# A decoder layer on one core: the first transposes of both attentions moved from TensorE to transposing DMAs

## The chip, the core and the metric

The kernel runs on one core of a Trainium2 chip. The metric is the device time of one execution in microseconds (us), lower is better. Engines by name: TensorE (PE; its weight loads are PEld), VectorE (DVE), ScalarE (ACT), GpSimd (POOL) and SyncE (SP), which here only issues DMAs. SBUF is the memory of 128 partitions that all engines work in, PSUM the one that TensorE writes to, in 8 banks.

## What is computed

One decoder layer on x, 16 batches of 128 tokens with 256 features, float32:

```
x = layernorm(x + differential_self_attention(x))   # 16 heads of 16, each split into two halves of 8
x = layernorm(x + cross_attention(x, ctx))          # 32 query heads of 8 over 8 key/value heads
x = layernorm(x + mixture_of_experts(x))            # 8 experts, 2 chosen per token, 2 shared ones
```

In the self attention queries and keys are rotated, each head's two halves give a softmax of their own, and the second is subtracted times a scalar lambda. Either attention therefore has 32 score matrices of 128 x 128 for a batch, with a depth of only 8:

```
scores = einsum(q, k) * scale (+ add_mask);  p = softmax(scores);  out = p @ v
```

## The kernel before

**Split numbers.** Float32 products are made from float16 pieces: a value is split into a high part (ScalarE, a cast) and a low part (GpSimd, the value less its high part). For a batch, the queries of an attention `t` (A self, C cross) lie in the tile `t.qs`, [128 tokens, 32 heads, 32 slots] f16: high, low, high, and one slot for the negated row maximum. The keys lie in `t.ks` in the same way. So a tile is 128 x 1024 f16, 256 KB.

**Two passes.** Scores are computed twice. `max_scores` (L942) makes them in 8 fills of 4 heads, VectorE takes the row maximum of each (`largest`, L678) and writes it into the query tile. Then the queries are transposed again, now with the maxima in them (`restack`, L936), and `exp_scores` (L955) computes scores less maximum, on which ScalarE takes the exponential (`exp`, L512). Both passes read tiles with the head dimension on the partitions: `t.qm` the queries of the first pass, `t.qt` those of the second, `t.kt` the keys of both.

**The transposes.** `stack_T` (L914) makes such a tile with 8 transposes of 128 x 128 on TensorE into one PSUM bank; ScalarE or VectorE copies the bank to SBUF (`qm_in`, `kt_in`, `reqt_in`). There are six for a batch: first queries, keys and second queries, for each attention. `stack_q` (L922) and `stack_k` (L930) are the first ones of queries and keys.

**The order.** The attention block is a software pipeline. Each engine has a function `body(n)`, written out by hand, that is run for n = 0 to 22; iteration n holds steps of several batches at once: x is projected and rotated for batch n, the first pass of the self attention is at batch n - 1, its second pass at n - 2, its output at n - 3, the cross attention's second pass at n - 4, and so on. The engines meet only at semaphores. PSUM banks are shared in rings: `RINGS` (L50) lists for each bank, or pair of banks, which results take turns in it, and `Turns.wait` makes TensorE wait until the result before has been read. The transposes of both attentions have turns in the single banks 4 and 5, with the projections and the routing.

In an iteration TensorE does, among the rest and in this order: `stack_q(A, n-1)` after the first scores of the second pass, `stack_k(A, n-1)`, `restack(C, n-4)`, `out_project(n-3)`, `max_scores(A, n-1, 0)`, ..., `values_cross(n-4, 0)`, `stack_k(C, n-3)`, `project_qk(n)`, `stack_q(C, n-3)`, `group_mean(n-2)`, `values_cross(n-4, 1)`, `restack(A, n-1)`, `max_scores(C, n-3, 0)`. `keep_warm` adds matmuls without a use where TensorE would idle, in the first and last iterations. GpSimd's low parts are `q_low` (L306), `k_low` (L312), `cross_k_low` (L324), `cross_q_low` (L318).

**SyncE.** It issues the loads at the start, then two pieces of the shared experts' weights, fills the DRAM tensor `xs` (39 tiles of 128 rows) with zeros by one DMA, loads four more weight pieces as their buffers come free, and waits for the zeros. The experts' part follows after the attention block, and the change doesn't touch it.

Of the kernel before, what the change touches and what calls it, by code (L numbers as in the profile page):

```python
# [56 lines left out]
    (1, (("aqT", 1, 0), ("akT", 1, 0), ("v", 1, 0), ("xT", 0, 0), ("qk", 0, 0), ("are", 1, 0))),  # L57
    (1, (("rt", 7, 0), ("cre", 4, 0), ("x2T", 6, 0), ("ckT", 3, 0), ("cqT", 3, 0))),
# [5 lines left out]
SHARED_HIGH = 3  # L64
LAST = B + 1
# [44 lines left out]
def build(nc, a, out):  # L110
    ctx = ExitStack()
    sems = ExitStack()
    with sems, ctx:
# [31 lines left out]
        def attention_tiles(p, vheads):  # L145
# [3 lines left out]
            t.qm, t.qt, t.kt = (sb(p + n, [P, NC, P], F16) for n in ("qm", "qt", "kt"))  # L149
# [9 lines left out]
            t.s_qT, t.s_kT, t.s_reT = sem(p + "qT"), sem(p + "kT"), sem(p + "reT")  # L159
# [70 lines left out]
        def live(b):  # L230
# [6 lines left out]
            "aqT": (A.s_qm_in, 1), "akT": (A.s_kt_in, 1), "are": (A.s_reqt, 1),  # L237
            "cqT": (C.s_qm_in, 1), "ckT": (C.s_kt_in, 1), "cre": (C.s_reqt, 1), "x2T": (A.s_x2lo, 1), "rt": (A.s_lgc, 1),
# [14 lines left out]
        def _(sp):  # L253
# [13 lines left out]
            sp.dma_start(x_all[:, 4:B, :], xv[:, 4:B, :]).then_inc(s_x[2], 16)  # L267

            sp.wait_ge(s_set, 4)
            for k in range(2):  # L270
                load_piece(sp, NE * 3 + k, k)
            sp.wait_ge(s_pset, 11)
            sp.dma_start(zero[:, E:E + 1], a["pad_row"]).then_inc(s_rowno, 16)
            sp.dma_start(x_row[:, :, E], a["acc_row"], allow_slow_non_contiguous=True).then_inc(s_rowno, 16)
            sp.wait_ge(s_rowno, 32)
            sp.dma_start(xs.rearrange("(n p) c -> p n c", p=P),
                         zero[:].unsqueeze(1).to_broadcast([P, TILES, RW])).then_inc(s_zero, 16)
            for k in range(2, NSH * 3):
                sp.wait_ge(s_xwlo, k - 1)
                load_piece(sp, NE * 3 + k, k)  # L280
            sp.wait_ge(s_zero, 16)
# [149 lines left out]
        def _(act):  # L431
# [34 lines left out]
            def k_high(b):  # L466

                act.activation(A.ks[:, :, 0:2 * SD].rearrange("p j (r d) -> p j r d", d=SD),
                               A.rq[:, E:2 * E].rearrange("p (j d) -> p j d", d=SD).unsqueeze(2)
                               .to_broadcast([P, SUB, 2, SD]), ACT.Copy).then_inc(A.s_khi, 1)  # L470
# [10 lines left out]
            def cross_k_high(b):  # L481

                if b == 0:
                    act.wait_ge(s_ctx, 16)
                else:
                    act.wait_ge(C.s_kT, b)
# [4 lines left out]

            def qm_in(t, one, b):

                act.wait_ge(t.s_qT, b + 1)
                act.activation(t.qm[:].rearrange("p c n -> p (c n)"), one.bitcast(F16), ACT.Copy
                               ).then_inc(t.s_qm_in, 1)

            def kt_in(t, one, b):

                act.wait_ge(t.s_kT, b + 1)  # L500
                if b:
                    act.wait_ge(t.s_expfill, FILLS * b)
                act.activation(t.kt[:].rearrange("p c n -> p (c n)"), one.bitcast(F16), ACT.Copy
                               ).then_inc(t.s_kt_in, 1)
# [30 lines left out]
            def body(n):  # L535
# [18 lines left out]
                if live(n - 1):  # L554
                    kt_in(A, a_one, n - 1)
# [22 lines left out]
                if live(n - 3):  # L578
                    cross_q_high(n - 3)
                    if n < LAST:  # L580
                        kt_in(C, c_one, n - 3)
# [3 lines left out]
                if live(n - 3) and n < LAST:  # L585
                    qm_in(C, c_one, n - 3)
# [15 lines left out]
        def _(dve):  # L602
# [57 lines left out]

            def qm_in(t, one, b):

                dve.wait_ge(t.s_qT, b + 1)
                dve.tensor_copy(t.qm[:].rearrange("p c n -> p (c n)"), one.bitcast(F16)).then_inc(t.s_qm_in, 1)

            def kt_in(t, one, b):

                dve.wait_ge(t.s_kT, b + 1)
                if b:
                    dve.wait_ge(t.s_expfill, FILLS * b)  # L670
                dve.tensor_copy(t.kt[:].rearrange("p c n -> p (c n)"), one.bitcast(F16)).then_inc(t.s_kt_in, 1)
# [115 lines left out]
            def body(n):  # L787
# [8 lines left out]
                if live(n - 1):  # L796
                    qm_in(A, a_one, n - 1)
# [45 lines left out]
                if live(n - 3) and n >= LAST:  # L843
                    kt_in(C, c_one, n - 3)
# [16 lines left out]
                if live(n - 3) and n >= LAST:  # L861
                    qm_in(C, c_one, n - 3)
# [13 lines left out]
        def _(pe):  # L876
# [45 lines left out]
            def stack_q(t, one, b):  # L922
# [3 lines left out]
                pe.wait_ge(t.s_qlo, b + 1)  # L926
                turns.wait(pe, "aqT" if t is A else "cqT", b)
                stack_T(t.qs, one, t.s_qT)

            def stack_k(t, one, b):  # L930

                pe.wait_ge(t.s_klo, b + 1)
                turns.wait(pe, "akT" if t is A else "ckT", b)
                stack_T(t.ks, one, t.s_kT)

            def restack(t, one, b):  # L936

# [4 lines left out]
            def max_scores(t, b, f):  # L942

                if f == 0:
                    pe.wait_ge(t.s_qm_in, b + 1)
                    pe.wait_ge(t.s_kt_in, b + 1)
                turns.wait(pe, "am" if t is A else "cm", b, f)
                r = slice(SLOTS * (f % 4), SLOTS * (f % 4) + USED)
                for j in range(NI):
                    c = NI * (f // 4) + j  # L950
                    ins = pe.matmul(score_bank(t, "m", b, f)[:, j * P:(j + 1) * P], t.qm[r, c, :], t.kt[r, c, :],  # L951
# [956 lines left out]
```

## Time and profile before

| | |
|---|---|
| median of 3 runs | 839.91 us (838.23 to 842.63) |
| the profiled execution | 839.69 us, its span 837.6 us |
| TensorE busy | 774.1 us, 92% |
| VectorE, ScalarE busy | 524.6 us (63%), 516.2 us (62%) |
| GpSimd busy | 309.3 us, 37% |
| mean granted clock of TensorE | 0.976 |

The span is the time from the first to the last instruction of the profiled execution; what its own time has more lies around it. Busy shares are means over both parts of the kernel, the attention block and the experts. The attention block ends at about 426 us.

### The profile page before, as it was taken

Reading aid. Unit: us, or ns where it says so; the run is one execution under the profiler, and the core shown is the slowest. Engines: PE = TensorE matmul, PEld = TensorE weight load, DVE = VectorE, ACT = ScalarE, POOL = GpSimd, SP = SyncE. Lnnn points to the kernel's source line nnn. Section 1 sums busy time; section 2 is a strip of 40 time slices with the busy share of each in tenths; the row PEclk is TensorE's granted clock in tenths of the full one; section 3 lists DMA queues with packets and bytes.
Section 4 is the critical chain, followed back from the end, with each engine's and each line's share of the span. In section 5 each row is a group of like instructions: output and inputs, shape, how many; then the busy total and the mean of one; then the engine's idle time right before and its main releaser. Section 6 shows DMA issues by size and latency. Waiting matters only on the chain. (4 is left out here: it accounts for less than half of the span.)

```text
span 837.6 us, 20147 instructions
## 1 busy us (share of the span) xinstructions
PE 774.1 (92%) x7698; PEld 512.9 (61%) x7698; DVE 524.6 (63%) x1193; ACT 516.2 (62%) x944; POOL 309.3 (37%) x480
## 2 busy tenths in 40 slices
PE   7888999999999999988889899989999999999993
PEld 5555555555555555555545555658888887788652
DVE  3346788888888888876448866764444444444353
ACT  2445788888888888774425554545565555565443
POOL 3134445555555555555200683002222222222222
PEclk9997999999999999999899999999999999999997
DMA  8900000001010100000033685432233233233321
GB/s 247 250 3 1 2 2 33 2 2 33 3 33 2 33 2 3 2 2 1 2 98 126 197 244 164 164 101 33 46 53 46 46 50 48 46 51 46 59 100 63
DMA packets 38282, 51.02 MB, mean 61 GB/s; under 512 B 9264, under 2 KB 33072, under 8 KB 38192
## 3 DMA queue, kind: packets, MB, share of 16 engines
q1 hardware_dynamic: 31040, 40.39, 16.3%
q0 software_dynamic: 7152, 9.34, 6.8%
q8 instruction: 66, 1.08, 0.5%
q14 instruction: 24, 0.20, 0.1%
HBM read 31.04 MB, written 18.68 MB: 59 GB/s over the span
## 5 line engine op out<-in xcount | busy, mean ns | idle before, releaser
L1392 POOL DMA_INDIRECT acc<-y_sb,xin x39 | 60.6, 1553 | 217.8 <-ACT y_sb L1460 217.8
L1713 PE MATMUL ps<-wr,xr_hi 128*128 x624 | 129.3, 299 | 0.0
L1431 ACT ACTIVATE th<-ps 128x384 f32<-128x384 f32 (+1 forms) x118 | 58.0, 491 | 109.8 <-PE ps L1713 104.9
L1713 PE MATMUL ps<-xg_hi,wsh 128*128 128x512 f16 x320 | 102.6, 383 | 4.6 <-DVE xg_lo L1578 4.6
L682 DVE TENSOR_REDUCE a_qs<-ps 128x4 f16<-128x512 f32 x128 | 85.2, 690 | 18.8 <-PE ps L951 17.9
L682 DVE TENSOR_REDUCE c_qs<-ps 128x4 f16<-128x512 f32 x128 | 84.4, 694 | 16.7 <-PE ps L951 15.3
L515 ACT ACTIVATE a_pt<-ps 128x512 f32<-128x512 f32 x128 | 74.7, 596 | 31.4 <-PE ps L968 29.5
L1713 PE MATMUL ps<-wr,xr_lo 128*128 x312 | 93.4, 299 | 0.0
L1585 DVE SCALAR_TENSOR_TENSOR th<-th,ps 128x384 f32<-128x384 f32 (+1 forms) x118 | 65.3, 554 | 33.4 <-ACT th L1431 33.2
L515 ACT ACTIVATE c_pt<-ps 128x512 f32<-128x512 f32 x128 | 69.7, 603 | 21.1 <-PE ps L968 20.8
L1672 DVE COPY ht<-ps 128x512 f16<-128x512 f16 x39 | 16.6, 425 | 94.0 <-PE ps L1792 94.0
L1713 PE MATMUL ps<-wr,ht 128*128 x585 | 70.5, 273 | 0.8 <-issue 0.7
L1713 PEld LDWEIGHTS ps<-wr,xr_hi 128*128 128x128 f16 x624 | 59.4, 98 | 18.2
L1713 PEld LDWEIGHTS ps<-wr,ht 128*128 128x128 f16 x585 | 56.8, 98 | 8.5 <-issue 1.6
L1713 PE MATMUL ps<-xg_lo,wsh 128*128 128x512 f16 x160 | 61.3, 383 | 0.0
L1713 PE MATMUL ps<-wsh,ht_hi 128*128 128x256 f16 x320 | 54.7, 273 | 3.7 <-DVE ht_lo L1590 3.4
L1590 DVE TENSOR_TENSOR hs<-th,hs 128x384 f16<-128x384 f32 x78 | 38.4, 492 | 29.0 <-ACT hs L1436 29.0
L1436 ACT ACTIVATE hs<-th 128x384 f16<-128x384 f32 x78 | 36.6, 470 | 31.9 <-DVE th L1585 31.9
L1713 PEld LDWEIGHTS ps<-xg_hi,wsh 128*128 128x128 f16 x320 | 31.6, 99 | 39.9 <-issue 5.9
L962 PE MATMUL ps<-mask,id 128*128 128x512 f16 x128 | 50.9, 398 | 3.3 <-ACT a_qt L509 3.3
L968 PE MATMUL ps<-a_qt,a_kt 32*128 32x128 f16 x512 | 51.8, 222 | 0.0
L968 PEld LDWEIGHTS ps<-a_qt,a_kt 32*128 32x128 f16 x512 | 29.2, 94 | 33.5 <-issue 33.5
(214 smaller groups left out, 1758.3 us busy)
## 6 DMA issues: line engine op xcount, KB each, us to landing
wst<-in_wx SPq DMA_DIRECT2D x30, 640.0 KB, 4.4
xs<-zero SPq DMA_DIRECT2D x1, 5031.0 KB, 19.8
xin<-xs SPq DMA_DIRECT2D x39, 129.0 KB, 2.1
acc<-x_row SPq DMA_DIRECT2D x4, 512.0 KB, 3.3
x_row<-acc SPq DMA_DIRECT2D x8, 256.0 KB, 5.2
out<-x_row SPq DMA_DIRECT2D x8, 256.0 KB, 2.1
x_row<-in_x SPq DMA_DIRECT2D x1, 1536.0 KB, 10.9
wst<-in_wqkvT SPq DMA_DIRECT2D x1, 768.0 KB, 4.3
```

Of the source, the lines that this page charges most:

```text
L515: act.activation(t.pt[:, f, :, :].rearrange("p j n -> p (j n)"), score_bank(t, "e", b, f), ACT.Exp, scale=(E // HEADS if t is A else SD) * ...
L682: dve.tensor_reduce(t.qs[:].rearrange("p (c i) s -> p c i s", i=NI)[:, c:c + 4, f % 4, USED], score_bank(t, "m", b, f).rearrange("p (j n) ...
L962: pe.matmul(o.rearrange("p (j n) -> p j n", j=NI), id16[:], mask4[:].unsqueeze(1).to_broadcast([P, NI, P]), start=True, stop=False, skip_g ...
L968: ins = pe.matmul(o[:, j * P:(j + 1) * P], t.kt[r, c, :], t.qt[r, c, :], start=t is C, stop=True, skip_group_check=t is A)
L1392: pool.indirect_dma_start(acc, bass.IndirectOffsetOnAxis(ap=row, axis=0), y_sb[:, n % 2, :], None, compute_op=ALU.add).then_inc(f_acc, 16)
L1431: act.activation(th[:, k % 2, 0:n], gate[:, k % 2, 0:n], ACT.Silu, scale=1.0 / WSCALE).then_inc(f_th, 1)
L1436: act.activation(dst, th[:, k % 2, 0:dst.shape[-1]], ACT.Copy).then_inc(f_hhi, 1)
L1585: dve.scalar_tensor_tensor(out=t, in0=t, scalar=1.0 / WSCALE, in1=up[:, k % 2, 0:n], op0=ALU.mult, op1=ALU.mult).then_inc(f_hid, 1)
L1590: dve.tensor_tensor(dst, th[:, k % 2, 0:dst.shape[-1]], hi, ALU.subtract).then_inc(f_hlo, 1)
L1672: dve.tensor_copy(ht[:, HALVES[1][0]:, :, :].rearrange("p j r n -> p (j r n)"), htp[1]).then_inc(f_hTin[1], 1)
L1713: ins = pe.matmul(o, l[x], r[y], start=(first and n == 0), stop=(last and n == m - 1), skip_group_check=not (first and last))
```

## The change

The first transposes of queries and keys, in both attentions, are made by a transposing DMA from SBUF to SBUF, issued by SyncE. The second transposes of the queries stay on TensorE. `qm_in` and `kt_in` and their turns in the banks are gone. `t.kt` has two buffers, taken by even and odd batches. SyncE now has a `body(n)` as the other engines do; the load of x for batches 4 to 15, the pieces of shared weights and the zeros, now 13 DMAs of 3 tiles, are issued between the transposes.

```diff
-    (1, (("aqT", 1, 0), ("akT", 1, 0), ("v", 1, 0), ("xT", 0, 0), ("qk", 0, 0), ("are", 1, 0))),
-    (1, (("rt", 7, 0), ("cre", 4, 0), ("x2T", 6, 0), ("ckT", 3, 0), ("cqT", 3, 0))),
+    (1, (("v", 1, 0), ("xT", 0, 0), ("qk", 0, 0), ("are", 1, 0))),
+    (1, (("rt", 7, 0), ("cre", 4, 0), ("x2T", 6, 0))),
...
+ZT = 3
...
-            t.qm, t.qt, t.kt = (sb(p + n, [P, NC, P], F16) for n in ("qm", "qt", "kt"))
+            t.qm, t.qt = (sb(p + n, [P, NC, P], F16) for n in ("qm", "qt"))
+            t.kt = sb(p + "kt", [P, 2, NC, P], F16)
...
-            sp.dma_start(x_all[:, 4:B, :], xv[:, 4:B, :]).then_inc(s_x[2], 16)
...
+            def turn(dst, src, done):
+                sp.dma_start_transpose(out=dst, in_=src[:].rearrange("p j s -> p (j s)")).then_inc(done, 16)
+            def stack_k(t, b):
+                sp.wait_ge(t.s_klo, b + 1)
+                if b >= 2:
+                    sp.wait_ge(t.s_expfill, FILLS * (b - 1))
+                turn(t.kt[:, b % 2, :, :], t.ks, t.s_kt_in)
+            def stack_q(t, b):
+                sp.wait_ge(t.s_qlo, b + 1)
+                if b:
+                    sp.wait_ge(t.s_maxfill, FILLS * b)
+                turn(t.qm[:], t.qs, t.s_qm_in)
...
+            def zero_rows(k):
+                if k == 0:
+                    sp.wait_ge(s_rowno, 32)
+                ts = slice(k * ZT, (k + 1) * ZT)
+                sp.dma_start(xs.rearrange("(n p) c -> p n c", p=P)[:, ts, :],
+                             zero[:].unsqueeze(1).to_broadcast([P, ZT, RW])).then_inc(s_zero, 16)
+            def shared_piece(k):
+                if k < 2:
+                    sp.wait_ge(s_set, 4)
+                else:
+                    sp.wait_ge(s_xwlo, k - 1)
                 load_piece(sp, NE * 3 + k, k)
...
+            def body(n):
+                if live(n - 1):
+                    stack_q(A, n - 1)
+                if live(n - 1):
+                    stack_k(A, n - 1)
+                if n == 1:
+                    sp.dma_start(x_all[:, 4:B, :], xv[:, 4:B, :]).then_inc(s_x[2], 16)
+                if live(n - 3):
+                    stack_k(C, n - 3)
+                if n == 2:
+                    shared_piece(0)
+                    shared_piece(1)
+                    row_numbers()
+                k, half = divmod(n - SHARED_HIGH, 2)
+                if half == 0 and 2 <= k < NSH * 3:
+                    shared_piece(k)
+                if 0 <= n - 3 < TILES // ZT:
+                    zero_rows(n - 3)
+                if live(n - 3):
+                    stack_q(C, n - 3)
```

The high parts of the next batch wait for the DMA that reads the key tile, where they waited for the transposes (`act.wait_ge(A.s_kt_in, 16 * b)` in `k_high`, and the same in `cross_k_high`). `max_scores(t, b, 0)` waits for both DMAs. The calls of `stack_q`, `stack_k`, `qm_in` and `kt_in` are taken out of the bodies of TensorE, ScalarE and VectorE; all else there keeps its place.

## Rows read from the trace of the kernel before

**Rows 1.** The page: span, busy time and its 40 slices.

```profile
span 837.6 us, 20147 instructions
...
PE 774.1 (92%) x7698; PEld 512.9 (61%) x7698; DVE 524.6 (63%) x1193; ACT 516.2 (62%) x944; POOL 309.3 (37%) x480
...
PEclk9997999999999999999899999999999999999997
```

**Rows 2.** Windows of 21 us: length, busy us (instructions) of each engine, PEclk, DMA share.

```profile
63.00:84.00 21.00, 18.00 (x170) 10.58 (x162) 13.92 (x33) 11.15 (x19) 8.81 (x17) 0.75 0.01 1
210.00:231.00 21.00, 19.76 (x274) 12.36 (x275) 17.55 (x43) 17.36 (x33) 11.25 (x20) 1.00 0.01 3
```

**Rows 3.** Timeline of GpSimd, the rotary sum of batches 4 and 15: start, us.

```profile
99.74 1.27 POOL L304 TENSOR_TENSOR a_rq<-a_rq,a_r 128x512 f32<-128x512 f32 x1
...
344.48 1.26 POOL L304 TENSOR_TENSOR a_rq<-a_rq,a_r 128x512 f32<-128x512 f32 x1
```

**Rows 4.** Timeline of TensorE in one steady iteration, matmuls only.

```profile
264.46 0.41 PE L951 MATMUL ps<-a_kt,a_qm 24*128 24x128 f16 x8
...
276.94 0.40 PE L951 MATMUL ps<-c_kt,c_qm 24*128 24x128 f16 x8
...
281.46 0.62 PE L919 MATMUL ps<-id,a_qs 128*128 128x128 f16 x8
281.92 0.38 PE L962 MATMUL ps<-mask,id 128*128 128x512 f16 x1
...
283.23 0.62 PE L919 MATMUL ps<-id,a_ks 128*128 128x128 f16 x8
...
286.70 0.41 PE L951 MATMUL ps<-a_kt,a_qm 24*128 24x128 f16 x8
```

**Rows 5.** Timeline of GpSimd in the same iteration: the low parts.

```profile
272.30 0.63 POOL L321 TENSOR_TENSOR c_qs<-x_row,c_qs 128x256 f16<-128x256 f32 x1 [0.82 <-ACT c_qs L477]
...
280.73 0.67 POOL L309 TENSOR_TENSOR a_qs<-a_rq,a_qs 128x256 f16<-128x256 f32 x1 [0.80 <-ACT a_qs L462]
...
281.55 0.67 POOL L315 TENSOR_TENSOR a_ks<-a_rq,a_ks 128x256 f16<-128x256 f32 x1
...
287.77 0.67 POOL L327 TENSOR_TENSOR c_ks<-ctx_all,c_ks 128x256 f16<-128x256 f32 x1 [4.76 <-ACT c_ks L488]
```

**Rows 6.** Timelines of ScalarE and VectorE in the same iteration: the copies out of PSUM.

```profile
272.90 1.02 ACT L503 ACTIVATE c_kt<-ps 128x1024 f16<-128x1024 f16 x1 [0.68 <-PE ps L968]
...
274.87 1.02 ACT L495 ACTIVATE c_qm<-ps 128x1024 f16<-128x1024 f16 x1
...
285.57 1.02 ACT L503 ACTIVATE a_kt<-ps 128x1024 f16<-128x1024 f16 x1
...
282.12 0.69 DVE L664 COPY a_qm<-ps 128x1024 f16<-128x1024 f16 x1 [0.35 <-PE ps L919]
```

**Rows 7.** The page, DMA issues: KB each, median us from issue to landing.

```profile
wst<-in_wx SPq DMA_DIRECT2D x30, 640.0 KB, 4.4
xs<-zero SPq DMA_DIRECT2D x1, 5031.0 KB, 19.8
...
x_row<-acc SPq DMA_DIRECT2D x8, 256.0 KB, 5.2
out<-x_row SPq DMA_DIRECT2D x8, 256.0 KB, 2.1
```

**Rows 8.** DMA view of 0 to 430 us, same columns.

```profile
wst<-in_woT SPq DMA_DIRECT2D x1, 256.0 KB, 3.5
...
ones<-in_ones SPq DMA_DIRECT2D x1, 32.0 KB, 1.9
...
x_row<-in_acc_row SPq DMA_DIRECT2D x1, 8.0 KB, 7.2
```

**Rows 9.** Timeline of SyncE's queue: start, and us that the issue itself took.

```profile
0.73 0.40 SPq L255 DMA_DIRECT2D x_row<-in_x  x1
...
8.46 1.90 SPq L267 DMA_DIRECT2D x_row<-in_x  x1
```

More of the change, by code:

```diff
@@ L236, in build @@
             "xT": (A.s_xlo, 1), "qk": (A.s_rdve, 3), "v": (A.s_vin, 1),
-            "aqT": (A.s_qm_in, 1), "akT": (A.s_kt_in, 1), "are": (A.s_reqt, 1),
-            "cqT": (C.s_qm_in, 1), "ckT": (C.s_kt_in, 1), "cre": (C.s_reqt, 1), "x2T": (A.s_x2lo, 1), "rt": (A.s_lgc, 1),
+            "are": (A.s_reqt, 1),
+            "cre": (C.s_reqt, 1), "x2T": (A.s_x2lo, 1), "rt": (A.s_lgc, 1),
             "apv0": (A.s_ot[0], 1), "apv1": (A.s_ot[1], 1), "cpv0": (C.s_ot[0], 1), "cpv1": (C.s_ot[1], 1),
@@ L266, in _ @@
             sp.dma_start(ctx_all[:], a["ctx"].rearrange("(b p) c -> p b c", p=P)).then_inc(s_ctx, 16)
-            sp.dma_start(x_all[:, 4:B, :], xv[:, 4:B, :]).then_inc(s_x[2], 16)
-            sp.wait_ge(s_set, 4)
-            for k in range(2):
-                load_piece(sp, NE * 3 + k, k)
-            sp.wait_ge(s_pset, 11)
-            sp.dma_start(zero[:, E:E + 1], a["pad_row"]).then_inc(s_rowno, 16)
-            sp.dma_start(x_row[:, :, E], a["acc_row"], allow_slow_non_contiguous=True).then_inc(s_rowno, 16)
@@ L275, in _ @@
[L275 to L281, printed above, removed]
+            def turn(dst, src, done):
+                sp.dma_start_transpose(out=dst, in_=src[:].rearrange("p j s -> p (j s)")).then_inc(done, 16)
@@ new lines, in stack_k, with row_numbers @@
+            def stack_k(t, b):
[8 more added lines that the diff above has]
+                turn(t.qm[:], t.qs, t.s_qm_in)
+            def row_numbers():
+                sp.wait_ge(s_pset, 11)
+                sp.dma_start(zero[:, E:E + 1], a["pad_row"]).then_inc(s_rowno, 16)
+                sp.dma_start(x_row[:, :, E], a["acc_row"], allow_slow_non_contiguous=True).then_inc(s_rowno, 16)
@@ L284, in _ @@
+            for n in range(ITERATIONS):
+                body(n)
+            sp.wait_ge(s_zero, 16 * TILES // ZT)
         @block.gpsimd
@@ L466, in k_high @@
             def k_high(b):
+                if b:
+                    act.wait_ge(A.s_kt_in, 16 * b)
                 act.activation(A.ks[:, :, 0:2 * SD].rearrange("p j (r d) -> p j r d", d=SD),
@@ L485, in cross_k_high @@
                 else:
-                    act.wait_ge(C.s_kT, b)
+                    act.wait_ge(C.s_kt_in, 16 * b)
                 for r in range(2):
@@ L490, in cross_k_high @@
                                    .to_broadcast([P, KV, GRP, SD]), ACT.Copy).then_inc(C.s_khi, 1)
[L492 to L504, printed above, removed]
             def reqt_in(t, one, b):
@@ L584, in body @@
                     exp(C, n - 4, 7)
-                if live(n - 3) and n < LAST:
-                    qm_in(C, c_one, n - 3)
                 if live(n - 4):
@@ L659, in rope_second @@
                                   ).then_inc(A.s_rdve, 1)
[L661 to L671, printed above, removed]
             def reqt_in(t, one, b):
@@ L842, in body @@
                     moments(A, A.bn, A.mv, n - 2, A.s_bn, A.s_mv)
-                if live(n - 3) and n >= LAST:
-                    kt_in(C, c_one, n - 3)
                 if live(n - 1):
@@ L860, in body @@
                     cross_moments(n - 5)
-                if live(n - 3) and n >= LAST:
-                    qm_in(C, c_one, n - 3)
                 if live(n):
@@ L920, in stack_T, with restack @@
                 ins.then_inc(s, 1)
-            def stack_q(t, one, b):
+            def restack(t, one, b):
                 if t is A and b == 0:
                     pe.wait_ge(s_const, 16 * N_CONST)
[L926 to L936, printed above, removed]
                 pe.wait_ge(t.s_maxed, FILLS * b + FILLS)
@@ L944, in max_scores @@
                 if f == 0:
-                    pe.wait_ge(t.s_qm_in, b + 1)
-                    pe.wait_ge(t.s_kt_in, b + 1)
+                    pe.wait_ge(t.s_qm_in, 16 * b + 16)
+                    pe.wait_ge(t.s_kt_in, 16 * b + 16)
                 turns.wait(pe, "am" if t is A else "cm", b, f)
```

20 lines of the change are left out of this document (3 added, 17 removed).

## The prediction

> **What bounds the kernel now.** I read the page first: TensorE is busy 92% of the span, VectorE and ScalarE little over 60%, and its granted clock is full nearly throughout [rows 1]. The change lies in the attention block alone, the first half of the span, so I went on to windows of that block. In a steady one of 21 us TensorE is busy 19.8, VectorE 17.6, ScalarE 17.4 [rows 2]: TensorE bounds it, but the other two have only 3.5 us to spare, so a wait put into the chain between them can't hide for long. The rotary sum of batch 4 starts at 99.74 and that of batch 15 at 344.48 [rows 3]: 11 iterations of 22.25 us. With the neighbours that are nearly as full, I count 13 steady iterations. Four batches are in flight, but every engine runs a fixed order, so the iteration is a ring of dependent steps, and I measured that ring with the timelines of one iteration [rows 4, 5]:
>
> - (a) cross max scores start 276.94, the low part of the self keys ends 281.55 + 0.67 = 282.22: 5.3 us
> - (b) from there to the self max scores at 286.70: 4.5 us
> - (c) self max scores at 264.46 to the end of the low part of the cross queries, 272.30 + 0.63 = 272.93: 8.5 us
> - (d) from there to the cross max scores at 276.94: 4.0 us
>
> The sum is 22.3, the period. In (b) and (d) a transpose and its copy out of PSUM are done today, between other work. These two gaps, 8.5 us together, are the room that a transposing DMA has before the period grows.
>
> **What is removed.** Four of the six transpose groups of an iteration leave TensorE. One occupies it from 281.46 to 281.92 [rows 4], 0.46 us for 8 transposes; four are 1.83 us. Three copies of 1.02 us leave ScalarE and one of 0.69 us leaves VectorE [rows 6]: with overlap about 2.8 and 0.6 us. With nothing waiting for a DMA, TensorE's own period would be 22.23 - 1.83 = 20.4: VectorE then has 18.6 - 0.6 = 18.0 of work (17.6 x 22.2/21 = 18.6) and ScalarE 15.6, so TensorE stays the bound. I split TensorE's work so: (a) + (b) less the two self groups, 9.76 - 0.92 = 8.8 us; (c) + (d) less the two cross groups, 12.48 - 0.92 = 11.6 us.
>
> **What is added.** Four DMAs an iteration on SyncE's queue, each 128 x 1024 f16, 256 KB. The trace has no transposing DMA, so landing time (L) and issue time (I) are bounded by its plain ones. L: 256 KB out of SBUF to HBM land in 2.1 us, 256 KB into SBUF in 5.2 (behind other traffic) and, as the weights of the projection, in 3.5 [rows 7, 8]. I take 3.3, close to the latter, a little less since nothing is queued ahead. I: the shortest issue takes 0.40 us, that of a load in 1,536 rows of 1 KB takes 1.90 [rows 9]; a transpose of 1,024 rows of 256 B lies between, I take 1.4. Waits in the order of SyncE's program: self queries (low part over at 280.73 + 0.67 = 281.40), then self keys (ready at 282.22), then cross keys (ready 288.44 [rows 5], wanted a full 10 us later: hidden), then cross queries. So the self keys are issued behind the self queries: issue 1.4 less the 0.8 between them is 0.6 us late. Gap (b) becomes L + 0.6 = 3.9, gap (d) L = 3.3. What waits there is TensorE at its first max scores, all in its order behind them (the values, the scores of the other attention, the next projection), and through them VectorE's maxima and ScalarE's exponentials.
>
> In (a) a late start no longer waits behind the second transpose's copy, and VectorE and ScalarE have no backlog: I shorten it by 0.4, to 4.9. In (c) VectorE's maxima run as before: 8.5, and 0.1 for the semaphore. The period is then the larger of 8.8 and 4.9 + 3.9 = 8.8, plus the larger of 11.6 and 8.6 + 3.3 = 11.9: 20.7. Gain 22.23 - 20.7 = 1.53; 13 x 1.53 = 19.9 us.
>
> The Trainium skill ("DMA: Bandwidth & Descriptors", Latency and other measured facts and its table of limits) gives a transposing DMA 261 GB/s, and some 2 us fixed for any DMA (Anatomy of one DMA). My estimate from that page is 1.0 + 2.0 = 3.0 us for 256 KB; the sum by it would be 20.4 a period, 4 us better in all. No row here shows a transposing DMA.
>
> **What moves.** The write of zeros was one DMA, 5,031 KB in 19.8 us [rows 7]; it is now 13 pieces of 387 KB, by the same row 1.5 us each, issued between cross keys and cross queries in 13 iterations. Alone it is done (288.5 + 1.4 + 1.5) long before the cross queries at 295.2. In four iterations a shared weight piece of 4.4 us [rows 7] stands ahead of it: 288.5 + 1.4 + 4.4 + 1.5 = 295.8, so the transposes behind it start up to a microsecond late: 4 x 1.0 = 4 us. (If the zeros held it up each time: 13 x 1.5 = 20 us; if never, 0.) The shared pieces are loaded later than before, but are used only at the end of the iteration: hidden. x of batches 4 to 15 goes behind the first two transposes; batch 4 is wanted three iterations on: nothing. The doubled key tile only takes away a wait. Start and drain: iterations 1 and 16 to 18 are chains of latency, where TensorE's transpose and copy took less than a DMA does; about 1 us later in two of them: 2 us. The experts are as before: 0.
>
> **Sum.** 839.7 (the profiled execution, span 837.6; the median of runs is 839.9) - 19.9 + 4 + 2 = 825.8: 826.
>
> **The rivals.**
>
> 1. *All hidden.* L is like the store's 2.1 us [rows 7], I near 0.4: period 20.4, 13 x 1.83 = 23.8, start and contention 1: 817. For it: a transpose reads and writes SBUF only. Against: every load in the rows took over 3 us for this size.
> 2. *A draw.* L = 3.9, still I = 1.4: 4.9 + 4.5 plus 8.6 + 3.9 = 21.9 a period; 13 x 0.33 = 4.3 gained, 6 lost: 841. This is the point from which it decides: above L of 3.7 nothing is left of the gain.
> 3. *Slower, TensorE waits for small pieces.* A DMA pays by the piece. The 8 KB of row numbers go in 2,048 pieces, 128 for each of 16 engines, in 7.2 us [rows 8]; against 1.9 for 32 KB of ones in the same rows that is 5.3/128 = 41 ns a piece. A transpose has 1,024 rows of 256 B, 64 to an engine: 64 x 41 ns = 2.6 us, L = 1.9 + 2.6 = 4.5, and the keys follow the queries 2.6 - 0.8 = 1.8 later. 4.9 + 6.3 plus 8.6 + 4.5 = 24.3: 13 x 2.1 = 27 lost, plus 6: 872. For it: those pieces did cost that. Against: they are 4 bytes each and strided in HBM. Waits of 2 us could also drop TensorE's clock, as in the window from 63 us, where it was busy only 18.0 us and was granted 0.75 [rows 2], that is half speed for half of the window; 3 us at half speed in each iteration would cost 13 x 1.5 = 20 us more, 892.
> 4. *Far slower, square block by square block.* A transpose is eight blocks of 128 x 128, 32 KB each; a 32 KB load takes 1.9 us [rows 8]. One after another they take up to 15 us, the keys 14 us behind: 4.9 + 29 plus 8.6 + 15 = 58 a period, 1,300 us. The Trainium skill ("VectorE: DVE Perf Modes", The three transpose paths) speaks against the change: it gives 1,309 ns for one such block by DMA, 390 on TensorE, and advises TensorE where the result may lie in PSUM. My estimate by that page is 8 x 1.3 = 10.5 us, a period of 44 and 1,125 us. Against: nothing says that the blocks don't overlap.
>
> **The numbers.** This kernel's runs spread over 838.2 to 842.6, so about 0.5% (4.2 us) is what can be told from no change. Chances: forecast 0.36 (its own range 819 to 835), rival 1 0.14, rival 2 0.14, rival 3 0.31, rival 4 0.05. Faster 0.50, same 0.14, slower 0.36. For 8 in 10 the range leaves out rival 4, the upper part of rival 3 with the clock, and a little of rival 1: 814 to 880.
>
> **What would show it.** Landing of the transposes in the DMA issues: under 3.7 right, over 3.9 wrong. Rotary sums 20.7 us apart. TensorE waiting for the queue at the max scores: about 0.3 us before the cross ones, near nothing before the self ones; if a microsecond or more stands before both, rival 3. Groups of L919 down from 768 to 256 matmuls, ScalarE's busy time down by some 44 us. The granted clock of the steady windows still 1.00. The prediction is wrong if the issue occupies SyncE for over 2 us, if a transpose holds up the DMAs around it, or if the ring was not (a) to (d).

## The result: a small gain where a larger one was forecast

The changed kernel takes 835.91 us in the median of 20 runs (828.14 to 840.4), the kernel before, beside it, 840.51 us (834.29 to 846.55). The ratio is 0.9936, interval 0.9909 to 0.9962: 0.6% faster, 4.6 us by the medians and 5.4 by the ratio. Forecast were 826 and a gain of 14. The profiled execution of the changed kernel took 836.23 us, its span 834.1. In two kernels below, e3_self_only and e7_edges_warm, one and two of 12 runs were in a slower state at a lower clock; those runs are left out below.

The page of the changed kernel: span, busy time of TensorE and ScalarE, TensorE's granted clock in 40 slices, against [rows 1].

```profile
span 834.1 us, 19099 instructions
...
PE 759.6 (91%) x7186; PEld 491.4 (59%) x7186; DVE 510.3 (61%) x1173; ACT 474.4 (57%) x900; POOL 309.9 (37%) x480
...
PEclk9787799999999999996699999999999999999998
```

ScalarE lost 41.8 us and VectorE 14.3. TensorE has 512 matmuls fewer, but the clock row shows 7, 8, 7, 7 in the second to fifth slices (9, 9, 7, 9 before) and 6, 6 in the two at the end of the attention block (9, 8 before). The execution's mean clock is 0.951 against 0.976.

The DMA issues of the changed kernel (KB each, median us from issue to landing), against [rows 7].

```profile
wst<-in_wx SPq DMA_DIRECT2D x30, 640.0 KB, 4.7
xs<-zero SPq DMA_DIRECT2D x13, 387.0 KB, 4.1
...
a_qm<-a_qs SPq DMA_TRANSPOSE x16, 3.2
a_kt<-a_ks SPq DMA_TRANSPOSE x16, 3.1
c_kt<-c_ks SPq DMA_TRANSPOSE x16, 3.5
c_qm<-c_qs SPq DMA_TRANSPOSE x16, 3.0
```

A transpose of 128 x 1024 f16 lands in 3.0 to 3.2 us in the median of three of the four kinds, and in 3.5 for the cross keys, whose issue itself often took longer. A piece of zeros took 4.1 us. SyncE's queue in one steady iteration (start, us of the issue):

```profile
254.24 1.23 SPq L272 DMA_TRANSPOSE a_qm<-a_qs  x1
255.57 1.29 SPq L272 DMA_TRANSPOSE a_kt<-a_ks  x1
259.71 2.51 SPq L272 DMA_TRANSPOSE c_kt<-c_ks  x1
262.27 0.57 SPq L299 DMA_DIRECT2D xs<-zero  x1
267.32 1.23 SPq L272 DMA_TRANSPOSE c_qm<-c_qs  x1
```

Timelines of GpSimd: the rotary sums of batches 1, 4 and 15 and, in between, the low parts of self keys and cross queries in that iteration, against [rows 3, 5].

```profile
31.96 1.27 POOL L357 TENSOR_TENSOR a_rq<-a_rq,a_r 128x512 f32<-128x512 f32 x1 [15.55 <-DVE a_r L685]
...
103.48 1.26 POOL L357 TENSOR_TENSOR a_rq<-a_rq,a_r 128x512 f32<-128x512 f32 x1
...
254.35 0.67 POOL L368 TENSOR_TENSOR a_ks<-a_rq,a_ks 128x256 f16<-128x256 f32 x1
...
266.66 0.64 POOL L374 TENSOR_TENSOR c_qs<-x_row,c_qs 128x256 f16<-128x256 f32 x1 [0.82 <-ACT c_qs L532]
...
334.56 1.26 POOL L357 TENSOR_TENSOR a_rq<-a_rq,a_r 128x512 f32<-128x512 f32 x1
```

From batch 4 to batch 15 the sums stand 231.08 / 11 = 21.0 us apart, each step between 20.98 and 21.18, against 22.25. So the steady part gained 13.7 us. The same rows tell where it went. Batch 4 starts 3.7 us later than in [rows 3]. Batch 0 starts 0.2 us later (13.02 against 12.80) and batch 1 4.5 us (31.96 against 27.42), so 4.3 us are lost between these two, and 0.8 are won back before batch 4. The end is the routing's softmax of the last batch, on VectorE, first of the kernel before:

```profile
426.09 0.24 DVE L1647 TENSOR_SCALAR sg<-lg 128x128 f32<-128x128 f32 x1 [0.33 <-PEq L1199]
```

and of the changed kernel:

```profile
420.98 0.24 DVE L1644 TENSOR_SCALAR sg<-lg 128x128 f32<-128x128 f32 x1 [0.33 <-PEq L1196]
```

From batch 15 to there it was 81.6 us and is 86.4: the drain lost 4.8. In all -13.7 + 3.7 + 4.8 = -5.1 us for the attention block (rounded). The experts, which the change leaves alone, took 1.6 us more in this execution (413.1 against 411.5).

**The steady iteration.** TensorE of the changed kernel, the rows that bound the ring, with the waits behind brackets, against [rows 4]:

```profile
254.52 0.39 PE L967 MATMUL ps<-mask,id 128*128 128x512 f16 x1 [0.36 <-ACT a_pt L556]
...
258.83 0.41 PE L956 MATMUL ps<-a_kt,a_qm 24*128 24x128 f16 x8
...
269.19 1.06 PE L1001 MATMUL ps<-c_pt,c_v 128*32 128x512 f32 x8 [0.68 <-DVE a_g L755]
...
270.75 0.41 PE L956 MATMUL ps<-c_kt,c_qm 24*128 24x128 f16 x8
```

No max scores wait here, neither the self ones at 258.83 nor the cross ones at 270.75. What TensorE waits for is ScalarE's exponential and VectorE's group statistics. Windows of one whole period show the account: before,

```profile
210.00:232.23 22.23, 20.99 (x284) 12.75 (x282) 18.78 (x47) 18.59 (x35) 12.19 (x23) 1.00 0.01 3
```

and after:

```profile
210.00:230.99 20.99, 19.21 (x251) 10.95 (x252) 18.00 (x46) 15.76 (x32) 12.16 (x23) 1.00 0.37 70
```

TensorE lost 1.78 us of work, about the 1.83 that were forecast, and its idle time grew from 1.24 to 1.78 us. The period shrank by the difference, 1.24.

**The edges.** In the attention block TensorE waits for a queue in only three places behind the first loads. They are the first self max scores and the cross max scores of batches 14 and 15:

```profile
20.66 0.41 PE L956 MATMUL ps<-a_kt,a_qm 24*128 24x128 f16 x8 [4.08 <-DMA a_kt<-a_ks]
...
374.61 0.41 PE L956 MATMUL ps<-c_kt,c_qm 24*128 24x128 f16 x8 [2.81 <-DMA c_qm<-c_qs]
...
394.15 0.62 PE L956 MATMUL ps<-c_kt,c_qm 24*128 24x128 f16 x8 [2.91 <-DMA c_qm<-c_qs]
```

Windows around them (length, busy us and instructions of each engine, PEclk, DMA share, GB/s), before:

```profile
20.00:30.00 10.00, 8.29 (x77) 5.69 (x78) 6.11 (x12) 1.79 (x3) 1.27 (x1) 1.00 0.81 217
...
390.00:400.00 10.00, 9.11 (x70) 5.25 (x69) 3.89 (x12) 3.93 (x8) 5.10 (x7) 0.72 0.01 2
400.00:410.00 10.00, 8.06 (x85) 5.17 (x84) 7.36 (x15) 2.17 (x4) 2.17 (x4) 0.84 0.01 2
```

and after:

```profile
20.00:30.00 10.00, 9.09 (x54) 4.78 (x55) 5.42 (x9) 0.77 (x2) 0.00 (x0) 0.56 0.50 157
...
63.00:84.00 21.00, 17.10 (x164) 9.53 (x166) 13.79 (x33) 9.63 (x18) 9.46 (x18) 0.73 0.27 60
210.00:231.00 21.00, 19.22 (x251) 10.96 (x252) 18.01 (x46) 15.77 (x32) 12.17 (x23) 1.00 0.37 70
...
390.00:400.00 10.00, 6.56 (x58) 3.36 (x56) 2.95 (x5) 2.46 (x5) 2.80 (x5) 0.67 0.15 28
400.00:410.00 10.00, 9.81 (x67) 5.96 (x69) 4.78 (x13) 3.19 (x7) 1.41 (x3) 0.50 0.00 0
```

Right behind the first wait the granted clock falls from 1.00 to 0.56: TensorE is busier there than before (9.09 against 8.29 us) and finishes 54 instructions instead of 77. The steady window stays at 1.00, and the dip of 63 to 84 us was there before (0.73 now, 0.75 in [rows 2]).

How much longer the wait itself became is read from the end of a low part to the max scores that need it. At the start, before (low part of the self keys, then the self max scores):

```profile
15.52 0.67 POOL L315 TENSOR_TENSOR a_ks<-a_rq,a_ks 128x256 f16<-128x256 f32 x1
...
19.03 0.41 PE L951 MATMUL ps<-a_kt,a_qm 24*128 24x128 f16 x8 [0.39 <-ACT a_kt L503]
```

and after, where the max scores are the row at 20.66 above:

```profile
15.74 0.67 POOL L368 TENSOR_TENSOR a_ks<-a_rq,a_ks 128x256 f16<-128x256 f32 x1
```

That is 2.84 us before and 4.25 after, 1.4 more. For cross batch 14, before and after (the max scores after are the row at 374.61):

```profile
381.16 0.67 POOL L321 TENSOR_TENSOR c_qs<-x_row,c_qs 128x256 f16<-128x256 f32 x1 [0.88 <-ACT c_qs L477]
...
384.38 0.41 PE L951 MATMUL ps<-c_kt,c_qm 24*128 24x128 f16 x8 [0.96 <-DVE c_qm L664]
```

```profile
370.82 0.67 POOL L374 TENSOR_TENSOR c_qs<-x_row,c_qs 128x256 f16<-128x256 f32 x1 [0.90 <-ACT c_qs L532]
```

This is 2.55 and 3.12 us, 0.6 more; for batch 15 it is 3.52 and 3.14, 0.4 less. So the three paths grew by 1.6 us together, though TensorE idles in them for 9.8 us: what it did there before (transposes, matmuls of `keep_warm`) overlapped them.

**Theories.** A: the steady part is worth what it shows, and the edges take it back, each wait by its own length and by the lower clock behind it. B: the steady gain is limited by the landing of the self keys or the cross queries. C: the moved loads and the zeros cost something of themselves. The first four kernels were aimed at A and at the split between the attentions, the next four at B and C and at a better version, the last three at A once more, by adding the waits to the kernel before.

### The profile page after: what moved, and what is told of

Same layout as the page of the kernel before. It is cut to its first block and busy times, and to the rows that moved or that the text cites. A ratio compares the mean times of both kernels' runs of the same rounds, so it can differ in the third digit from the quotient of the medians.

```text
span 834.1 us, 19099 instructions
## 1 busy us (share of the span) xinstructions
PE 759.6 (91%) x7186; PEld 491.4 (59%) x7186; DVE 510.3 (61%) x1173; ACT 474.4 (57%) x900; POOL 309.9 (37%) x480
## 5 line engine op out<-in xcount | busy, mean ns | idle before, releaser
L556 ACT ACTIVATE c_pt<-ps 128x512 f32<-128x512 f32 x128 | 69.8, 603 | 22.3 <-PE ps L973 21.6
```

The costliest lines, as they stand in the source:

```text
L556: act.activation(t.pt[:, f, :, :].rearrange("p j n -> p (j n)"), score_bank(t, "e", b, f), ACT.Exp, scale=(E // HEADS if t is A else SD) * ...
```

## Experiments on the edges and on each attention alone

For four of these kernels the first transposes can be put back on TensorE batch by batch. The core of the edit; the copies `qm_in` and `kt_in`, and the turns in the PSUM rings, are those of the kernel before:

```diff
+def on_pe(p, kind, b):
+
+    return 0 <= b < B and (...)
...
             def stack_k(t, b):
 
+                if on_pe(t.p, "k", b):
+                    return
                 sp.wait_ge(t.s_klo, b + 1)
...
                     exp_scores(A, n - 2, 5)
+                if on_pe("a", "k", n - 1):
+                    stack_k(A, a_one, n - 1)
```

**e1_warm: more matmuls of no use ahead of the three waits.**

```diff
                 if n == 1:
-                    keep_warm(8)
+                    keep_warm(8 + 30)
...
                 if n >= LAST and live(n - 3):
+                    keep_warm(24, a_one)
                     max_scores(C, n - 3, 0)
```

> The changed kernel, with 30 more warming matmuls ahead of the first self max scores and 24 more ahead of the cross max scores of the last two batches, the three places where its trace shows TensorE waiting for a transposing DMA (4.1, 2.8 and 2.9 us). Theory A: the waits cost most through the clock, which falls to half after them; filled, the clock stays at 2.4 GHz, the three waits still last, and the time falls by about 5 us against the changed kernel, to some 831 us (0.988 of the kernel before); the second rotary sum comes at 29 to 30 us in place of 32.0. Theory B: the waits cost by their own length only; nothing is gained, 0.994.

Measured: 837.3 us (829.46 to 840.22, 12 runs) against 841.94 of the kernel before; ratio 0.9942 (0.9905 to 0.9978), the same as for the change itself. The three waits shrank to 1.7, 1.1 and 0.4 us (a new one, of 1.5 us for the self queries, stood before the self max scores of batch 15). At the start this did not help: the window of 20 to 30 us still had a low clock, 0.60, and batch 1 started at 32.42. In the drain it did, in the one trace: from batch 15 to the end the granted clock was 0.92 and the time 84.0 us, against 0.82 and 86.4 in the change. That execution's attention block ended 3.5 us sooner than the change's, at 417.46, but its experts, which are the same in both, took 4.6 us longer, for no reason found. The mean clock rose to 0.964 in the average of the runs (0.956 for the change), without a gain in the whole time. The 5 us that theory A expected are not there, and filling the first wait this far was not enough.

**e2_edges: no transposing DMA at the edges.** `on_pe` is true for self batch 0 and for cross batches 14 and 15.

```diff
+    return 0 <= b < B and ((p == "a" and b == 0) or (p == "c" and b >= B - 2))
```

> The changed kernel with the first transposes of self batch 0 and of cross batches 14 and 15 given back to TensorE and their copies; all others by DMA. Theory A (the steady iterations gained 13.7 us, and start and drain gave back 3.7 and 4.8): the second rotary sum at 27.5 us, the attention block over at about 413 us, 0.984 of the kernel before, 827 us. Theory B (what is lost at the start and at the end comes of the moved loads and zeros on the same queue, or of the shorter steady iteration itself): the block is over at 418 us or later, 0.990 or more.

Measured: 829.52 us (826.45 to 831.74, 6 runs), ratio 0.987 (0.9828 to 0.9912). TensorE waits for no queue; batch 1 starts 14.71 us behind batch 0 (14.62 in the kernel before, 18.94 in the change), the steady steps are 20.99, the block ends at 414.40. So the three waits of the change are worth 5 to 6 us of its time (by the ratios 5.5, and 5.0 with e11_edges_again below). One iteration of the profiled execution took 25.49 us instead of 21, with this in its windows:

```profile
120.00:123.00 3.00, 2.69 (x37) 1.28 (x33) 2.69 (x5) 2.64 (x6) 2.19 (x6) 1.00 0.00 0
123.00:133.00 10.00, 9.87 (x74) 5.41 (x78) 5.53 (x14) 3.83 (x9) 3.89 (x7) 0.51 0.43 85
```

No queue was waited for there: the clock can fall in a steady iteration too, and this fall cost 4.5 us.

**e3_self_only and e4_cross_only: one attention by DMA.**

```diff
+    return 0 <= b < B and (p == "c")
```

for the self attention by DMA alone, and for the cross attention alone:

```diff
+    return 0 <= b < B and (p == "a")
```

> Only the self attention's first transposes by DMA, the cross ones on TensorE as before. If TensorE's work sets the period: 0.92 us off it, 21.3 us an iteration. If a ring of dependent steps sets it, whose gaps shrank only where a DMA took the place of transpose and copy: near 21.6. One wait of 4.1 us at the start stays, so 0.991 to 0.995 of the kernel before.

> Only the cross attention's first transposes by DMA. TensorE's work: 21.3 us a period; ring: near 21.7. The two waits in the drain stay (4.8 us given back), the start is as before: 0.992 to 0.997 of the kernel before.

Measured: e3_self_only 836.12 us (833.48 to 843.66, 11 runs), ratio 0.9967 (0.9934 to 1.0), steady steps mostly of 21.55 us; e4_cross_only 839.92 us (837.01 to 844.32, 12 runs), ratio 0.9983 (0.9955 to 1.001), steps of 21.74 and 21.84. Against 22.23 that is 0.68 and about 0.44 us for the halves, and 1.24 for both: within 0.12 the halves add up. Both are nearer to what the ring gave (21.6 and 21.7) than to the 21.3 of TensorE's work. In the whole time neither half can be told from no change with certainty: both intervals reach 1.0. The self half pays its wait of 4.0 us at the start, the cross half its two in the drain, 5.7 us together.

## Experiments on what sets the steady period

**e5_late_keys: the self keys 1.3 us later.**

```diff
                 if live(n - 1):
                     stack_q(A, n - 1)
+                if 5 <= n <= 14:
+                    sp.wait_ge(s_spare, 16 * (n - 5))
+                    sp.dma_start_transpose(out=spare[:], in_=wq_hi[:].rearrange("p c n -> p (c n)")[:, 0:NC * P]
+                                           ).then_inc(s_spare, 16)
                 if live(n - 1):
                     stack_k(A, n - 1)
```

> The changed kernel with one more transposing DMA of the same size (128 x 1024 f16, of constant weights into a spare tile) on SyncE's queue between those of the self queries and the self keys, in iterations 5 to 14. The self keys are then issued 1.2 to 1.3 us later. Theory (the ring through the landing of the self keys sets the period): the rotary sums of these iterations stand 22.2 us apart instead of 20.99, and TensorE shows a wait, perhaps not named as one for the queue, of about 1.2 us more before the self max scores. Rival (TensorE's own work sets the period, and the landing has slack): the period grows by less than 0.4 us. The whole kernel by the theory: 10 x 1.2 = 12 us more, about 848.

Measured: one run, 846.02 us, with steps of 22.3 us (22.26 to 22.40). In its timeline TensorE now waits before the self max scores:

```profile
222.12 0.41 PE L962 MATMUL ps<-a_kt,a_qm 24*128 24x128 f16 x8 [1.20 <-issue]
```

The keys were issued 2.70 us behind the queries instead of 1.33, so 1.37 later. Of that 1.20 became a wait and 1.3 a longer period: the landing of the keys has under 0.2 us of slack.

**e6_work_ahead: 0.4 us more work for TensorE ahead of the self max scores.**

```diff
                 if n == 1:
                     keep_warm(8)
+                if 5 <= n <= 14:
+                    keep_warm(4, a_one)
                 if live(n - 1):
                     max_scores(A, n - 1, 0)
```

> The changed kernel with 4 matmuls of no use ahead of the self max scores in iterations 5 to 14, 0.4 us of TensorE's work an iteration that is ready before the keys land. Theory (the landing of the self keys sets gap (b)): they lie in the wait, the period stays at 20.99 within 0.1. Rival (TensorE's work sets the period): it grows by the whole 0.4, to 21.4.

Measured: steps of 21.40 us (21.39 to 21.41 where nothing disturbed them), so the work was paid in full: TensorE's order is the bound. With e5_late_keys this makes a tie, as far as one run of each can show it. TensorE comes to the self max scores just when the keys land: issued at 255.57, 3.1 us to land, 258.67, and the max scores at 258.83. A delay on either side lengthens the period. Theory B holds for the limit, not as a present wait.

The run took 852.02 us, more than 4 us of added work explain, and one step took 27.54 us. There a landing came late, 4.6 us instead of 3.0, and the row and the window behind it are these:

```profile
189.03 0.41 PE L956 MATMUL ps<-c_kt,c_qm 24*128 24x128 f16 x8 [1.12 <-DMA c_qm<-c_qs]
```

```profile
191.00:204.00 13.00, 13.00 (x104) 7.13 (x104) 7.10 (x15) 6.30 (x13) 4.82 (x8) 0.50 0.32 62
```

A wait of 1.1 us was followed by 13 us at 0.50, the lower of the two clock levels, and the step grew by 6.1.

**e8_moves_only: the rest of the change.** All first transposes on TensorE, but SyncE's loads and zeros moved and two key tiles.

```diff
+    return 0 <= b < B and (True)
```

> The rest of the change without the transposing DMAs: all first transposes on TensorE with their copies out of PSUM, but the loads and the zeros of SyncE moved as in the change, and two key tiles. Theory (the moved transfers are hidden and cost nothing): period 22.2, ratio to the kernel before 1.000 within 0.003. Rival (the moved loads or the 13 pieces of zeros cost something of themselves): the period or the start is longer, ratio above 1.004.

Measured: 840.84 us (834.39 to 843.57, 12 runs) against 841.96, ratio 0.9994 (0.9974 to 1.0014). The rotary sums of batches 4 and 15:

```profile
94.92 1.27 POOL L374 TENSOR_TENSOR a_rq<-a_rq,a_r 128x512 f32<-128x512 f32 x1
...
340.64 1.26 POOL L374 TENSOR_TENSOR a_rq<-a_rq,a_r 128x512 f32<-128x512 f32 x1
```

That is 22.34 us a step, 0.1 more than before, and no difference in the whole that the 12 runs can tell. Theory C falls. Batches 0 and 1 start at 12.82 and 27.53, as before, so the moves have no part in the late start either.

**e7_edges_warm: e2_edges with more matmuls of no use** in iteration 3 (24) and at the start of the last full iteration (12).

```diff
+                if n == LAST - 1:
+                    keep_warm(12, a_one)
...
-                if 1 <= n < 3:
+                if 1 <= n < 4:
                     keep_warm(8)
...
-                if 1 <= n < 3:
+                if 1 <= n < 4:
                     keep_warm(16)
```

> The kernel of e2_edges (first transposes of self batch 0 and of cross batches 14 and 15 on TensorE, all others by DMA) with more matmuls of no use where TensorE stood idle: 24 in iteration 3 and 12 at the start of the last full iteration. Theory (idle time at the edges lets the clock fall, and that gave back the gain): the clock stays at 1.00 through iterations 3 and 4, mean clock 0.975 or more, median about 825. Rival (the clock falls where it falls, whatever TensorE does in the few us before): no better than e2_edges, 829.5, mean clock 0.965.

Measured: 834.0 us (827.09 to 837.7, 10 runs) against 841.96, ratio 0.9906 (0.9878 to 0.9933): no better than e2_edges. The clock did rise, 0.981 in the mean of these runs, but of the 10 steady steps from batch 5 on only three were 20.99 us; the others were 22.1 to 22.5. In those 7 the self queries came late:

```profile
238.27 0.41 PE L1025 MATMUL ps<-a_kt,a_qm 24*128 24x128 f16 x8 [1.46 <-DMA a_qm<-a_qs]
```

Their landing took 4.9 us in the median here, and 3.2 in the change and in e2_edges, for the same transfer issued at the same place of the iteration. Both sizes occur in e1_warm, e3_self_only and e6_work_ahead too (longest 4.5, 5.0 and 5.3 us). What holds it up was not found.

## Experiments that add the waits to the kernel before

The surest test of theory A leaves everything on TensorE and adds only the waits, by a transposing DMA into a spare tile. Two pieces of weights and the zeros, behind it in SyncE's queue, are issued 5 to 6 us later by it; e8_moves_only moved them too, without a cost that can be told, and had 1.00 in the window of 20 to 30 us.

**e9_before_waits: all three waits.**

```diff
+            def late(done, count):
+
+                sp.wait_ge(done, count)
+                sp.dma_start_transpose(out=spare[:], in_=wq_hi[:].rearrange("p c n -> p (c n)")[:, 0:NC * P]
+                                       ).then_inc(s_spare, 16)
...
+            late(A.s_kt_in, 1)
             sp.wait_ge(s_set, 4)
...
+            for i in (1, 2):
+                sp.wait_ge(s_spare, 16 * i)
+                late(C.s_qm_in, B - 2 + i)
...
                     pe.wait_ge(t.s_qm_in, b + 1)
+                    if t is A and b == 0:
+                        pe.wait_ge(s_spare, 16)
+                    if t is C and b >= B - 2:
+                        pe.wait_ge(s_spare, 16 + 16 * (b - B + 3))
```

> The kernel before, all its first transposes on TensorE, with the three waits of the changed kernel put in: TensorE waits ahead of the first self max scores, and of the cross max scores of batches 14 and 15, for a transposing DMA into a spare tile that is issued when the copy out of PSUM is done. Theory (a wait of TensorE at the edges costs itself and lowers the granted clock behind it): 3 waits of some 3.2 us are 9.6, the mean clock falls by 0.01 or more, and another 5 us go there: some 855 against 840.5, with clocks of 0.5 to 0.8 right behind the waits. Rival (the clock's dips are not made by the waits): 9.6 us at most, 850 or less, mean clock as before within 0.003.

Measured: 859.15 us (854.89 to 860.44, 6 runs) against 840.73, ratio 1.0211 (1.0177 to 1.0245): 18.4 us for three waits. TensorE's rows with them, the last two put down to nothing by name, since another wait stands between:

```profile
22.61 0.62 PE L968 MATMUL ps<-a_kt,a_qm 24*128 24x128 f16 x8 [3.53 <-DMA spare<-wq_hi]
...
390.94 0.62 PE L968 MATMUL ps<-c_kt,c_qm 24*128 24x128 f16 x8 [4.16 <-issue]
...
414.05 0.50 PE L968 MATMUL ps<-c_kt,c_qm 24*128 24x128 f16 x8 [3.94 <-issue]
```

The waits are 11.6 us together. The mean clock of the runs fell from 0.974 to 0.962. Within each kernel's runs the time goes with the clock: a straight line through time over mean clock falls by 5.8 us for each 0.01 in the 20 runs of the change, by 5.6 in the 17 of the kernel before here, by 6.0 in the 6 of this kernel (4.3 to 6.8 in the others). So the clock is worth about 1.2 x 5.8 = 7 us. The kernel before has waits of its own at these places, 0.4, 1.0 and 0.8 us, so 9.5 us of waiting were added. 9.5 + 7 = 16.5 is most of the 18.4 by the medians, 17.2 by the means. The added waiting alone can't explain it, and the rival's bound of 850 is passed.

**e10_before_first_wait: the first wait alone** (the line `late(A.s_kt_in, 1)` and TensorE's first condition).

> The kernel before with only the first of these waits, ahead of the first self max scores. Theory (a wait lowers the clock behind it): 3.2 us for the wait and some 4 for the clock between 20 and 32 us: about 848. Rival (the wait alone): 3.2 us, about 843.7, the granted clock from 20 to 32 us still 1.00.

Measured: 846.38 us (842.53 to 849.47, 12 runs) against 840.73, ratio 1.0062 (1.0038 to 1.0086): 5.7 us for a wait of 3.52. Batch 1 started at 33.72, 6.3 us later than before. The window that stood at 1.00 in the kernel before:

```profile
20.00:30.00 10.00, 7.60 (x50) 4.36 (x51) 4.97 (x9) 0.77 (x2) 0.00 (x0) 0.61 0.72 177
```

The first max scores stood 5.97 us behind the low part of the keys, 3.1 more than in the kernel before, and the step from batch 0 to batch 1 grew by 6.2, so 3.1 us lie behind the wait. Only the wait was added, with the DMA that makes it. Against a fall by such a DMA itself speak the steady windows of the change, at 1.00 with four of them in each iteration. The traces of all 13 kernels agree: in the seven whose TensorE waits for a queue before the first max scores (1.7 to 4.1 us) the window of 20 to 30 us has 0.52 to 0.66, in the six others it has 1.00. Theory A is shown for this place.

**e11_edges_again: e2_edges once more**, beside the two above.

> The kernel of e2_edges once more (first transposes of self batch 0 and of cross batches 14 and 15 on TensorE, all others by DMA), beside the two others on one chip. Theory (this is the version that keeps the gain of the steady part and loses nothing at the edges): ratio to the kernel before 0.985 to 0.990, iterations 20.99 apart. Rival (its landings vary as in e7_edges_warm, where 4.9 us were seen for the self queries): some iterations 22.5 apart, ratio 0.990 to 0.994.

Measured: 832.52 us (827.0 to 833.58, 6 runs) against 840.73, ratio 0.9877 (0.9838 to 0.9916), steady steps of 20.99. The two measurements agree, 0.987 and 0.9877. This version beats both kernels: 1.2 to 1.3% faster than the kernel before and some 0.6% faster than the change.

The second half of the theory, nothing lost at the edges, is not borne out by its profiled execution. The step from batch 1 to batch 2 took 26.79 us (24.22 before), and from batch 15 to the end it took 88.2 us (81.6 before, 86.4 in the change) at a granted clock of 0.81, with no wait for a queue. Over all traces the drain took 86.4 to 90.8 us at 0.81 to 0.89 in the five kernels whose TensorE waits there for a queue, 1.3 to 4.2 us before the cross max scores of either batch. It took 80.5 to 82.6 us at 0.92 to 0.94 in six of the seven kernels without such a wait; this one is the seventh. So in the drain the waits go with the fall, but a fall comes without them too.

## Why the prediction was wrong in size

The forecast was 826, a gain of 14; measured were 4.6 to 5.4. The time, 835.9, lies inside the range of 814 to 880 and just outside the likeliest case's own, 819 to 835. The sign and the mechanism of the steady part were right, its size and the terms beside it were not. Point by point, in the profiled executions, where the span fell by 3.5 us against 13.9 forecast:

- **Landing and issue: right.** L was taken as 3.3 and is 3.0 to 3.2 where the ring needs it; I was taken as 1.4 and is 1.23 to 1.29 for most. The sign of 2 us on SyncE did come for the cross keys, in 4 of 16 iterations, where it was hidden. Rivals 3 and 4 fall by the landing alone. The Trainium skill ("VectorE: DVE Perf Modes", The three transpose paths) gives 1,309 ns for one 128 x 128 block; that eight blocks cost eight times as much was my own step, an estimate of 10.5 us, and here they landed in 3.1. No run here shows a single block. The Trainium skill's rate of 261 GB/s ("DMA: Bandwidth & Descriptors", Latency and other measured facts) with the 2 us fixed of the same page (Anatomy of one DMA, which gives them for DMAs issued by GpSimd) gave an estimate of 3.0 us, and the trace, of DMAs issued by SyncE, agrees.
- **The ring: right in place, 0.3 us short.** Measured are (a) 5.27, (b) 3.81, (c) 8.47, (d) 3.45, together 21.0, against 4.9, 3.9, 8.6 and 3.3. (a) did not shorten by 0.4: it was 5.3 and stays so, and the backlog that I saw VectorE and ScalarE freed of was not what set it. The forecast TensorE wait of 0.3 us before the cross max scores isn't there; TensorE's idle time grew by 0.54 us in waits for the exponential and the group statistics instead. The period is 20.99, not 20.7, which over 11 steps is 3 us.
- **The number of steady iterations: 13 claimed, 11 measured.** Of the neighbours that I counted in addition, the step ahead of batch 4 went from 26.84 to 26.00 us, and the one behind batch 15 belongs to the drain, which lost; both are in the sums of start and drain below. (The first of them says little: this step took 23.92 us in e8_moves_only and 27.11 in e10_before_first_wait.) The two steps too many are 3 us, and with the size of a step this term is 11 x 1.24 = 13.7 instead of 19.9: 6.2 us of the miss.
- **Contention, 4 us: none.** The steps with a weights piece are as long as the others, and e8_moves_only shows no cost of the moves that can be told. That gives 4 us back. The zeros did take longer than I had them, 4.1 us to land and not 1.5, but they had room: in the iteration shown above the zeros are issued at 262.27 and the transpose behind them at 267.32, 5 us later.
- **Start and drain, 2 us: the step that failed.** I wrote that these are chains of latency, "about 1 us later in two of them". They lost 3.7 and 4.8 us, 8.5 together: 6.5 us of the miss. The latencies I had about right: the three paths grew by 1.4 + 0.6 - 0.4 = 1.6 us. What I put at nothing is the other 6.9 us. I priced a wait by the difference of two latencies, and left out that TensorE's clock falls behind it. The clock stood in the text only as part of rival 3, for steady iterations that wait. It belonged to the edges of the forecast itself: there the wait is bare, since no other batch's work fills it. At the start the fall is shown to be the wait's work: 4.3 us were lost between batches 0 and 1, 1.4 by latency and 2.9 behind it, where the granted clock was 0.56, and e10_before_first_wait lost 3.1 us behind a wait at the same place. In the drain the clock was 0.82 from batch 15 to the end, against 0.94 before, and latency is 0.2 of the 4.8 us; that the waits cause it there is likely, but e11_edges_again had 0.81 without them.
- **The experts, 0:** 1.6 us more in this execution. Their length varies between executions of one kernel as the clock does, and no run here ties it to the change.

These account for it: 6.2 - 4 + 6.5 + 1.6 = 10.3, and the difference of the spans is 13.9 - 3.5 = 10.4.

In the mean over the runs the clock points the same way. It is 0.956 in the 20 runs of the change (mean time 835.1) and 0.974 in the 29 of the kernel before that ran beside the first four experiments (841.1). At 5.8 us for 0.01 these 0.018 are 10.4 us, and at an equal clock the change would stand near 825. e2_edges, with its mean of 829.3 at 0.9655, comes to 829.3 - 0.85 x 5.8 = 824.4 by the same sum. That this sum may be made across kernels is argued, not shown: the 5.8 is a slope within one kernel. That it meets my 826 is luck. The steady gain less the longer latencies, 13.7 - 1.6 = 12.1, makes 829, so 4 us of the sum have no known source; and 826 held 6.2 too much gain and a loss of 4 that never came. It is also not shown why the clock is lower in e2_edges than before: it has no wait for a queue, only 0.5 us more of short waits in each iteration.

Rival 1 (817) falls with the 3.1 us landing and the waits above. Rival 2, the draw, came nearer to the time than the forecast did, but its reason, L of 3.9, was wrong. (Its remark that nothing is left of the gain above an L of 3.7 was loose too: by my own sum 3.5 us are left there, and nothing at 3.8.) Of what I named as signs, landing, the 256 matmuls of the second transposes, ScalarE (41.8 us against 44) and the steady clock came as said; the rotary sums (20.99) and the wait before the cross max scores did not.

## What to carry to other kernels

Before work is moved from TensorE to a queue, divide the places of use in two: those where other batches' work covers the landing, and the first and last ones, where nothing does. Keep the second kind on TensorE; here three batches out of 32 doubled the gain. Price a bare wait of TensorE by how much later its end comes and by the clock behind it, taken from a run with only that wait added (3.5 us cost 5.7). And when two paths come within a few tenths of a microsecond, as TensorE's order and the landing of the keys do here, test both with a small delay on each: neither shows as a wait in the trace.

## What the runs showed of the hardware

- A DMA transpose of 128 x 1024 f16 from SBUF to SBUF landed in 3.0 to 3.2 us and mostly took SyncE 1.23 to 1.29 us to issue. The keys of the cross attention, for no reason found, took up to 2.51 us to issue in the change, at a time when SyncE's last DMA before them had landed, and 3.5 us to land in the median.
- The same transfer at the same place landed in 4.5 to 5.3 us in some iterations, in e7_edges_warm in 7 of 10.
- After a wait of 1.12 us in a steady iteration TensorE ran 13 us at 0.50 and lost 6 us (e6_work_ahead); after one of 1.46 us in e7_edges_warm it stayed at 1.00 in the windows of 2 us behind it. In e2_edges the clock fell to 0.51 with no such wait. Nor was there one in the drain of e11_edges_again, at 0.81. At the start the two went together in all 13 kernels: a wait for a queue of 1.7 to 4.1 us and 0.52 to 0.66 behind it, or no such wait and 1.00.
